# A shorter softplus, decays as two one-pass halves, and a new order of calls in a kernel pipelined over four engines

## What is computed

```python
h = _s4d_kernel(log_dt, x, B, inv_A_real, A_imag, 1024)    # 2 * Re(sum_n C V), V = exp(dtA * l)
h = concatenate([cls_tok, h]); h = h + attn(layernorm(h)); h = h + ffn(layernorm(h))

# attn: down-projection to 128, gelu, hydra layer (twice), gate, up-projection
zxbcdt = u @ in_w.T
dt_fw = softplus(dt2[..., :NH] + dt_bias)                   # and dt_bw with the flipped half
xBC = silu(causal_conv(xBC, conv_w, conv_b))                # 7 taps
A = -exp(A_log)
h = exp(dt * A) * h + dt * x * B;  y = h . C                # forward and backward, shifted and added
y = y + xs * repeat(xs @ fcD_w.T + D);  yz = y * silu(z)
y = yz * rsqrt(mean(yz ** 2) + 1e-5) * norm_w;  out = y @ out_w.T

# ffn: dense 1024 x 1024 and LoRA experts
probs = softmax(x @ router_W.T + router_b)                  # 15 logits
topk_p, topk_i = top_k(probs, 8);  w = sum_k topk_p * onehot(expert_map[topk_i])
out = x @ base_W.T + base_b + ((x @ A.T) * w) @ B.T * 2
```

## Time and profile before

| | us |
|---|---|
| median of 3 runs (2546.2 to 2549.94) | 2546.23 |
| the profiled execution, device time | 2549.21 |
| its span, first to last instruction | 2547.5 |
| PE busy | 2236.7 (88%) |
| DVE busy | 1993.2 (78%) |
| ACT busy | 1529.7 (60%) |
| POOL busy | 1038.7 (41%) |

### The profile page before, as it was taken

How to read it: one execution, slowest core, us unless ns; L and a number is a source line. 1 busy time by engine, 2 the same in 40 slices (tenths; PEclk the granted TensorE clock), 3 DMA queues, 4 the chain that set the end, 5 groups by cost and what they waited for, 6 DMA issues and landing times.

```text
span 2547.5 us, 52475 instructions
## 1 busy us (share of the span) xinstructions
PE 2236.7 (88%) x14117; PEld 1838.9 (72%) x14117; DVE 1993.2 (78%) x5213; ACT 1529.7 (60%) x2926; POOL 1038.7 (41%) x1365
## 2 busy tenths in 40 slices
PE   1136799999999999999999999999999999999998
PEld 1125577777777777777777777777777777777776
DVE  6846788888878788888888787888888888878664
ACT  3435576666666666666666666666666666666652
POOL 2634444444444344444444343444444443434321
PEclk9966699999999999999999999999999999999999
DMA  3211011111111111111111111111111111111211
GB/s 102 71 34 33 33 52 37 59 58 58 58 38 49 58 58 58 55 31 58 58 58 58 38 49 58 58 58 55 32 58 58 58 58 38 49 58 57 63 36 31
DMA packets 90062, 132.62 MB, mean 52 GB/s; under 512 B 20379, under 2 KB 63559, under 8 KB 90006
## 3 DMA queue, kind: packets, MB, share of 16 engines
q1 hardware_dynamic: 79176, 125.60, 16.6%
q10 hardware_dynamic: 10830, 6.35, 0.9%
HBM read 55.17 MB, written 76.74 MB: 52 GB/s over the span
## 4 chain that ended last, share of the span: by engine, by line
PE 35%; DVE 23%; issue 21%; ACT 12%; DVEq 2%; POOL 1%; ACTq 1%; DMA 0%; SPq 0%; POOLq 0%
PE bank L1457 8%; PE bank L1556 5%; DVE sp_x L1129 3%; DVE NF L1192 3%; DVE NF L1198 3%; PE bank L1661 3%; PE bank L1546 3%; ACT T L877 3%; ACT CX L892 2%; DVE W L1157 2%; ACT SQ L975 2%; DVEq L47 2%; PE bank L1512 2%; PE bank L1487 2%; PE bank L1499 2%
## 5 line engine op out<-in xcount | busy, mean ns | idle before, releaser
L1457 PE MATMUL bank<-w_hi,XHI 128*128 128x512 f32 (+1 forms) x1560 | 629.2, 403 | 1.4 <-DVE XLO L1348 1.4
L1457 PE MATMUL bank<-w_lo,XHI 128*128 128x512 f32 (+1 forms) x1560 | 554.3, 355 | 0.0
L1457 PE MATMUL bank<-w_hi,XLO 128*128 128x512 f32 (+1 forms) x1560 | 553.9, 355 | 0.0
L1095 DVE SCALAR_TENSOR_TENSOR CX<-bank,cw,CX 128x252 f32<-128x252 f32 (+5 forms) x804 | 342.9, 461 | 100.8 <-ACT CX L892 100.8
L877 ACT ACTIVATE T<-bank 64x512 f32<-64x512 f32 x256 | 151.8, 593 | 352.8 <-PE bank L1546 348.2
L1457 PEld LDWEIGHTS bank<-w_hi,XLO 128*128 128x128 f32 x1560 | 295.6, 189 | 46.4
L1457 PEld LDWEIGHTS bank<-w_hi,XHI 128*128 128x128 f32 x1560 | 296.5, 190 | 38.3 <-DVE XLO L1348 1.7
L1457 PEld LDWEIGHTS bank<-w_lo,XHI 128*128 128x128 f32 x1560 | 296.3, 190 | 38.1
L849 POOL TENSOR_TENSOR CB<-CB,CM 48x252 f32<-48x252 f32 (+5 forms) x402 | 267.6, 666 | 137.9 <-ACT CM L877 109.2
L792 POOL TENSOR_TENSOR NB<-GB,sp_dt 128x512 f32<-128x512 f32 x67 | 100.3, 1496 | 297.4 <-DVE GB L1175 297.4
L813 POOL TENSOR_TENSOR RS<-VE,half_neg 128x1 f32<-128x1 f32 x65 | 35.6, 547 | 409.7 <-DVE VE L1292 409.7
(11 more groups left out here) (296 smaller groups left out, 5786.9 us busy)
## 6 DMA issues: line engine op xcount, KB each, us to landing
carried<-T SPq DMA_DIRECT2D x65, 512.0 KB, 4.7
T<-carried SPq DMA_DIRECT2D x65, 512.0 KB, 3.9
out<-HB SPq DMA_DIRECT2D x129, 256.0 KB, 3.2
tables<-tab SPq DMA_DIRECT2D x8, 560.0 KB, 4.1
TB<-tables SPq DMA_DIRECT2D x64, 70.0 KB, 2.8
carried<-U SPq DMA_DIRECT2D x65, 64.0 KB, 3.6
XM<-carried SPq DMA_DIRECT2D x65, 64.0 KB, 4.7
XI<-in_x SPq DMA_DIRECT2D x128, 32.0 KB, 2.8
```

The source lines that it names most:

```text
L1095: inc(STT(CX[:, c, :, s:CS], src[:, :, 0:CS - s], cw[:, c, k:k + 1], CX[:, c, :, s:CS], ALU.mult, ALU.add), "conv")
L1457: ins = mm(bank[:, 0:c1 - c0], xs_[:, 1 - p, k, :], ws[:, k, c0:c1], start=(c0 == HID and k == 0 and n == 0), stop=(last == k and n == 2))
```

## The change

It does four things. softplus has a polynomial of five coefficients (LOG1P, with the factor 2 in them) in place of nine, and takes the maximum in its last step: 13 steps instead of 18. The router keeps the unnormalised exponentials through top-8 and weights, and multiplies by the reciprocal of their sum in its last step: 9 steps instead of 10. The decays dt * A are split into a high half in F32R (AS[:, 0]) and the rest (AS[:, 1]); RF and RB are masked for each half, and decay_sums has eight F32R products in place of four F32 ones. The calls of PE, DVE, ACT and POOL stand in another order, and the two copies of swap are one.

```diff
-        earlier = sb("earlier", [P, P])
-        later = sb("later", [P, P])
+        earlier = sb("earlier", [P, P], F32R)
+        later = sb("later", [P, P], F32R)
...
+                link(dve.tensor_copy(earlier[:, :], earlier0[:, :]))
+                link(dve.tensor_copy(later[:, :], later0[:, :]))
...
-        RF = sb("RF", [P, 2 * NH, CS])
-        RB = sb("RB", [P, 2 * NH, CS])
+        RF = sb("RF", [P, 2, 2 * NH, CS], F32R)
+        RB = sb("RB", [P, 2, 2 * NH, CS], F32R)
+        AS = sb("AS", [P, 2, 2, 2, NH], F32R)
...
                         elif j == 6:
-                            ins = TS(f["p"], f["w"], 1.0 / 17, None, ALU.mult)
-                        elif j < 14:
-                            ins = STT(f["p"], f["p"], 1.0 / (29 - 2 * j), f["w"], ALU.add, ALU.mult)
-                        elif j == 14:
-                            ins = STT(f["p"], f["p"], 1.0, f["z"], ALU.add, ALU.mult)
-                        elif j == 15:
-                            ins = TS(f["x"], f["x"], 0.0, None, ALU.max)
-                        elif j == 16:
+                            ins = TS(f["p"], f["w"], LOG1P[4], None, ALU.mult)
+                        elif j < 10:
+                            ins = STT(f["p"], f["p"], LOG1P[10 - j], f["w"], ALU.add, ALU.mult)
+                        elif j == 10:
+                            ins = STT(f["p"], f["p"], LOG1P[0], f["z"], ALU.add, ALU.mult)
+                        elif j == 11:
                             wait(dve, q - 1, nb=1)
-                            ins = STT(f["dt"], f["p"], 2.0, f["x"], ALU.mult, ALU.add)
-                        elif j == 17:
-                            wait(dve, q - 1, rf=1, rb=1)
+                            ins = STT(f["dt"], f["x"], 0.0, f["p"], ALU.max, ALU.add)
+                        elif j == 12:
...
+                    def split_decays(part):
+
+                        if H:
+                            if part == 0:
+                                wait(dve, q, dtc=NDT)
+                                wait(dve, r, rb=2, rf=2)
+                                inc(dve.tensor_copy(AS[:, 0], SP16["aa"][:, :, :, :]), "asp")
+                            else:
+                                wait(dve, q, asp=1)
+                                inc(TT(AS[:, 1], SP16["aa"][:, :, :, :], AS[:, 0].bitcast(F32), ALU.subtract), "asp")
...
-                            wait(pe, r, rf=1, rb=1, sz=1)
+                            wait(pe, r, rf=2, rb=2, sz=1)
                             for a in range(2):
-                                for n, (m, dec) in enumerate(((earlier, RF), (later, RB))):
+                                for n, (m, dec) in enumerate(((earlier, RF), (earlier, RF), (later, RB), (later, RB))):
                                     ins = mm(bZ[:, 256 * a:256 * (a + 1)], m[:, :],
-                                             dec[:, NH * a:NH * (a + 1), :].rearrange("p h t -> p (h t)"),
-                                             start=(n == 0), stop=(n == 1))
+                                             dec[:, n % 2, NH * a:NH * (a + 1), :].rearrange("p h t -> p (h t)"),
+                                             start=(n == 0), stop=(n == 3))
```

More of the change, by code:

```diff
@@ L34 @@
 ROUND = float(1.5 * 2 ** 23)
+LOG1P = tuple(2.0 * c for c in (1.0000000039603822, 0.3333315734222377, 0.20012455115301675, 0.1398030151610831,
+                                0.14089167577571976))
 class Step:
@@ L265, in _ @@
                 pool.memset(ones[:, :], 1.0).then_inc(s_pool, 1)
-                for t in (ident, earlier, later):
+                for t in (ident, earlier0, later0):
                     pool.memset(t[:, :], 0.0).then_inc(s_pool, 1)
@@ L273, in _ @@
                     pool.wait_ge(s_masks, 1 + 4 * b)
-                    for dst, cols, sign in ((earlier, r, 1), (later, r, -1), (m_gt, slice(0, CS), 1),
+                    for dst, cols, sign in ((earlier0, r, 1), (later0, r, -1), (m_gt, slice(0, CS), 1),
                                             (m_lt, slice(0, CS), -1)):
@@ L664, in v3, with decays @@
             return ap.rearrange("p (a b) -> p a b", b=b)
-        def decays(d):
-            return SP16["aa"][:, d, :, :].rearrange("p a h -> p (a h)").unsqueeze(2).broadcast_to([P, 2 * NH, CS])
+        def decays(d, part):
+            return AS[:, part, d, :, :].bitcast(F32).rearrange("p a h -> p (a h)").unsqueeze(2) \
+                .broadcast_to([P, 2 * NH, CS])
         LOOP_FROM, LOOP_TO, LAST = 8, CLS - 2, TILES + 5
@@ L752, in body, with swap @@
                     q, r, td = i - 1, i - 2, i - 4
-                    def swap(k):
+                    def swap():
                         if A:
@@ L1068, in body @@
                     silu_bc(1)
+                    split_hi(1)
                     gelu()
-                    split_hi(1)
                 iterations(act, body)
@@ L1361, in final @@
                             inc(TT(HB[:, 1 - p, c], bO[h][:, :], HB[:, 1 - p, c], ALU.add), "fin")
+                    kernel_p()
                     gram(0)
                     gram(1)
-                    skip_scale()
-                    kernel_p()
+                    kernel_sum()
                     gram_forth()
@@ L1390, in body @@
-                    router(1)
                     stats_1(3)
-                    conv(4, 0)
+                    router(3)
                     conv(4, 1)
-                    router(2)
+                    conv(5, 0)
+                    router(4)
+                    router(5)
+                    softplus(0)
+                    softplus(1)
+                    residual(0)
+                    router(6)
+                    softplus(2)
                     shift_1()
-                    residual(0)
@@ L1397, in body @@
-                    softplus(0)
-                    router(3)
-                    softplus(1)
+                    softplus(3)
+                    router(7)
                     stats_2(0)
-                    softplus(2)
-                    router(4)
-                    softplus(3)
                     residual(1)
                     softplus(4)
-                    router(5)
+                    stats_2(1)
                     softplus(5)
-                    stats_2(1)
                     softplus(6)
-                    router(6)
+                    conv(5, 1)
@@ L1423, in body @@
-                    softplus(13)
-                    conv(5, 1)
-                    softplus(14)
-                    conv(6, 0)
-                    softplus(15)
                     shift_2()
-                    softplus(16)
+                    conv(6, 1)
+                    split_decays(0)
                     weighted_lo()
-                    softplus(17)
-                    conv(6, 1)
-                    decays_forth()
+                    split_decays(1)
+                    decays_forth(0)
```

153 lines of the change are left out of this document (77 added, 76 removed).

## The result

The changed kernel takes 2569.62 us (median of 4 runs, 2567.92 to 2571.25) against 2548.09 for the kernel before (2546.2 to 2550.21): ratio 1.0084, 95% interval 1.0067 to 1.0102. The forecast was 2398. Its profiled execution took 2567.92 us with a span of 2566.2.

What follows compares the result with a forecast made beforehand. PE's own stream was taken as the bound: 31.6 us plus stalls of 0.6 and 0.4 gives about 32.65 per period against 35.03, 148 us less in all, and 3.0 less for the median: 2398 us, range 2330 to 2490.

Steps and rivals of the forecast that it cites:

- 2.35 saved in each of about 60 full periods: The sum over the loop: periods of 32.6 to 32.7 us against 35.03, saving 141 us in the full periods.
- D: Rival: POOL's queue goes over its limit, NB starts late and the period passes 35.03; 2582 us, chance 0.07.
- decay_sums: forecast 0.96 for eight products: PE's decay sums: eight F32R products of 256 columns at 0.12 us each replace 1.64 us, saving 0.7.
- The stream was laid at 31.6: PE's work per period without stalls: 32.3 us less 0.7 for decay_sums and 0.1 for one precision change fewer.
- The stalls forecast at mix (0.6) and project_x (0.4): PE reaches mix at 7.5 before Mt at 8.1, and project_x at 10.4 before XD's sum at 10.8.
- Mt was laid to end at 8.1: The chain from gram through NB, NF, WI and W takes 4.5 us from 3.5 into the iteration.
- POOL's queue over the border: Decays, CB sum, T, swap and V, 6.7 us from 4.2 before the border, end 2.5 into the next iteration.
- NB was to start between 3 and 5: Sign in the profile after: NB on POOL starting before 3 or after 5 us would show the forecast wrong; 4.1 expected.
- the 1.49 us step: DVE's separate maximum of 16 elements in softplus, beside POOL's T; the profile after was to show it gone.
- the stalls of s4d(0) and project_out: PE's waits before these two groups, 0.5 to 0.9 and 0.4 us, were both to go.
- lora(0)'s: PE's stall of 1.1 us before lora(0) was to go, with 0.4 to 0.5 of cover.
- priced the decays by turns: RF on DVE (0.6) and RB on POOL (1.04) exclude each other: 3.3 us of both engines against 1.65.

Runs made afterwards that it cites:

- at slot 0: The changed kernel with the first instruction of DVE's loop laid at the start of a block of 128 instructions: 2374.94 us, 0.9319 of the kernel before.
- the same order: The changed kernel, DVE's loop at the start of a block, with full-precision decays instead of split halves: 2530.57 us, 0.9929 of the kernel before.
- the kernel before at slot 100: The kernel before with only DVE's loop head moved, to instruction 100 of a block of 128, touching four blocks: 2679.18 us, ratio 1.0509.
- with the hint: The changed kernel, its loop not placed, with hint_back_edge=True on DVE's loop: 2375.94 us, 0.932 of the kernel before.
- one wait added to the new order: The new order with full-precision decays (2530.57 us), plus a wait of POOL's decays_back for NM of shift_2: 2427.53 us, 0.9532 of the kernel before.

## Why the prediction was wrong, by its own steps

**The step that failed** is in the sum: "2.35 saved in each of about 60 full periods". It took every period of the loop for one like those of the trace before and had no term for the return to the loop's head. In the written-out iterations the saving was there (34.2 to 31.8 and 32.4), in the loop it became a loss of 0.8 (35.84 against 35.03). None of the rivals had this mechanism; D had the sign, by POOL's queue, which was in fact shorter than laid out. The page of before could not have shown the standstill, since nothing was fetched in its loop. It did show where to ask: 31 packets in the instruction queue for a DVE program in a loop of 54 iterations mean that the trip is held whole, and the change alters the length of that engine's code.

**With that taken away**, at slot 0, the time is 2375 us, inside the range and 23 below the forecast. Term by term:

- decay_sums: forecast 0.96 for eight products, measured 1173.45 to 1174.47, 1.02 us; 0.12 each was nearly right (0.13).

```profile
1173.45 0.48 PE L1644 MATMUL bank<-RF,earlier 128*128 128x256 f32 x2
1173.78 0.39 PE L1644 MATMUL bank<-RB,later 128*128 128x256 f32 x2
1174.01 0.39 PE L1644 MATMUL bank<-RF,earlier 128*128 128x256 f32 x2
1174.23 0.40 PE L1644 MATMUL bank<-RB,later 128*128 128x256 f32 x2
1174.47 0.27 PE L1578 MATMUL bank<-ident,XI 128*128 128x128 f32 x1
```

- The stream was laid at 31.6. The period is 32.08, with 0.3 of stall at lora(0) by distance from start to start and nothing measurable at mix, s4d(0), project_x, turn_x and project_out: so the stream is about 31.8.
- The stalls forecast at mix (0.6) and project_x (0.4) are not there. Mt was laid to end at 8.1, and ends 6.9 into the iteration; mix runs at 7.7, when PE gets to it. The mis-sized term is POOL's queue over the border: V was laid to end at 2.5 and ends at 1.8. kernel_p took its turn behind V, as forecast: VB starts 0.37 us before V's end at 1173.46 and ends 0.56 after it, so that its 0.93 is a wait and then the 0.6 of the forecast. The 0.7 goes on to gram and NB, and the chain from there to Mt took 4.1 instead of 4.6:

```profile
1173.09 0.93 DVE L1152 TENSOR_TENSOR VB<-TB 128x512 f32<-128x512 f32 x1
1173.94 0.27 DVE L1180 TENSOR_TENSOR GF<-bank,m_lt 128x126 f32<-128x126 f32 x1
...
1172.41 1.05 POOL L779 TENSOR_TENSOR V<-TB 128x512 f32<-128x512 f32 x1
1174.49 1.42 POOL L803 TENSOR_TENSOR NB<-GB,sp_dt 128x512 f32<-128x512 f32 x1 [1.02 <-DVE GB L1183]
```

- NB was to start between 3 and 5 and starts at 2.8. By the forecast's own signs this is a miss, and it is part of the reason why the stalls stayed away.
- gelu ends at 2.45 (forecast 2.55) and costs turn_x nothing; swap takes 0.28 (0.45); the 1.49 us step is gone; the stalls of s4d(0) and project_out went, and lora(0)'s fell from 1.1 to 0.3, where none was forecast.
- The decays begin 4.2 before the border, as laid, and do take turns: two RF in 2.13 us, RB in 1.43 and 1.03. But the turns are not alternating. A short DVE operation can stand through one POOL operation (1.47 beside T) or three (2.25), by whether POOL leaves a gap of 0.15 us. The forecast priced the decays by turns and gave NM nothing; that it fell well there, at 0.63, is luck: it is owed to the wait for AS, which I had not weighed, and without it the same order took 34.41 us per iteration.

What stays open: why the standstills differ in length. All end 1.4 to 1.7 us after a packet has landed; they differ by when it starts. In the 2.5 us ones it starts 0.4 to 0.8 us after DVE's last operation, in the long ones (3.6 on average ahead of GF in the change, 3.6 in the kernel before at slot 100) 1.1 to 2.3 us after it. What delays it isn't shown. Of the versions tried, the change with its loop at slot 0 is the fastest, 2374.94 us, 6.8% under the kernel before; with the hint it is the same within 0.4%.

## What to carry to other kernels

An edit that only shortens code can move an engine's loop over the edge of a block of instructions: compare the packets of the instruction queue and the "issue" waits of the loop's first instructions before and after (the chain's share of issue doesn't tell), before explaining a lost gain by data or order, and place the loop's head or hint its branch. Test the parts of a change in both orders of calls, and look at what joins them: here each seemed worth next to nothing, or less, without the other, until one wait added to the new order showed 2.1 us per iteration for the order and 0.7 for the halves. Where a short VectorE operation takes over a microsecond, look at the GpSimd queue beside it: removing that operation hands the time to the next one, a gap in the queue takes it away.

## What of the hardware was not expected

- A DVE loop of 312 or 329 instructions runs without a fetch, behind its first trip, when it touches three blocks of 128 instructions, and fetches five blocks per trip of 67 to 75 us when it touches four, even by 8 instructions. Each return then costs one standstill of 2.5 or 3.6 us, or two of 2.5 and 3.6, each ending 1.4 to 1.7 us after a packet has landed; the whole time differed by 67 to 195 us in a kernel of 2375 us.
- A hint on the branch (one instruction) removed fetches and standstill with the loop in four blocks: 2454 to 2384 us.
- A DVE standstill of 6 us stopped PE for 5, and then the clock went from the 2.4 to the 1.2 GHz level for 6.8 us: the 32 products of mix took 1.97 us instead of 1.15.
- One element per partition took 0.63, 1.47 or 2.25 us on DVE, by what POOL did meanwhile.
